# Expert loops with the up products' inner channels along partitions: no transposes of gated rows, and weights copied by ScalarE and VectorE

## The chip, the cores and the metric

One NeuronCore of a Trainium2 chip runs the whole program. The metric is the device time of one execution in microseconds. TensorE, VectorE, ScalarE, GpSimd and SyncE each run their own instruction stream and meet at semaphores. The profile calls them PE (its weight loads PEld), DVE, ACT, POOL and SP.

## The reference

Four sequences of 1024 tokens with 128 channels go through a mixing layer, a softmax attention, the mixing layer again, an expert layer, a linear attention and the expert layer again. The change is in the expert layer, which runs twice. Cut to what matters, for each token it computes:

```
up = moe_linear(xf, ids, w_up)            # 128 -> 512 channels, by the token's expert
u, gate = jnp.split(up, 2, axis=-1)       # two halves of 256
h = u * jax.nn.silu(gate)
down = moe_linear(h, ids, w_down)         # 256 -> 128 channels
```

Each token picks 2 of 8 experts, and all of it is float32.

## The kernel before, in words

The tokens are cut in rounds of 20, 12, 16 and 16 tiles of 128 tokens (SIZES); rounds 0 and 1 are the first pass through the expert layer, 2 and 3 the second. In each round every token's row is scattered twice to slots in HBM that are sorted by expert and padded to whole tiles of 128 rows, so that a tile has one expert. That gives 47, 31, 39 and 39 tiles, 156 in all. A loop (pe_loop, dve_loop, act_loop, pool_loop, sp_loop, one per engine) walks over them in units of two tiles: 24, 16, 20 and 20 units, 80 in all, the last of each round with one tile. The expert's weights lie in SBUF for all experts side by side (`k.expert_w`, in the trace `stack`), and a tile finds its expert's columns by an offset that a value_load (TENSOR_LOAD, with ISA instructions for registers) fetches from `moe_offsets`.

Iteration u of PE's loop does, in this order:

- loads the two offsets of unit u, and `turn(u)`: two transposes of the gathered rows (L1745) into bank 0; DVE scales them to `d.gt` (L1827, the trace calls the buffers lin_scores);
- side pieces of `k.e_plan` (first), which are other stages' work at fixed places: the end of the first attention and mixing, routing of the next round, preparation of the linear attention, and adding up the results of the round before (L1623, L1625);
- `up(u-1)`: for each tile one product with `d.gt` as weights (stationary) and 512 columns of the expert's up weights as moving operand (L1755). Its result has tokens along partitions. ACT takes silu of the gate half (L1861), DVE multiplies (L1834) into `d.h`;
- side pieces (second);
- `turn_hidden(u-2)`: four transposes of `d.h` (L1767) into bank 6, which ACT copies to `d.ht` (L1867);
- `down(u-3)`: four products of 128 columns (L1781) into bank 7, which ACT copies out (L1874). SP stores them to `results` (L1929) and, in its own order, loads the slots of units ahead (L1923).

SP's loads of the next round stand behind the last store of this one. POOL sends the scatters of the next round (L1689) and the gathers of the round before (L1700) as side pieces, and before each waits for PE to reach the same slot of the plan (pool_follow). Each engine takes its work in program order, so an iteration is as long as the slowest of what must be done in it. Between round 1 and round 2 lies the linear attention. After round 3 its 32 last gathers follow.

The key lines of the part that goes away, in pe_loop and act_loop:

```
instruction = T.transpose(k.ps[:, bank, at:at + P], d.h[:, u % NB, i, c * P:(c + 1) * P], k.ident[:, :])
...
A.activation(d.ht[:, u % NB, 0:width, :].rearrange("p i c -> p (i c)"), k.ps[:, bank, 0:width * HIDDEN],
             ACT_FN.Copy).then_inc(k.free[bank], 1)
```

## Time and profile before

| | |
|---|---|
| median of 3 runs | 1231.58 us (1227.18 to 1231.7) |
| the profiled execution: its own time / its span | 1228.77 us / 1227.0 us |
| PE busy | 1023.1 us, 83% |
| ACT busy | 798.9 us, 65% |
| DVE busy | 602.1 us, 49% |
| POOL busy | 428.5 us, 35% |
| first and last up product (L1755) of rounds 0 and 1 | from 633 us to 788 us |
| the same of rounds 2 and 3 | from 1030 us to 1171 us |

The span is from the first to the last instruction, the own time has what lies around it. Busy PE is not yet bound PE: matmuls overlap, and their ends are modelled. The chain of work that ended last says more: in it each piece stands with the time that it alone held up the end. A group of instructions has a count (x), a mean and the idle time before it with what ended it.

### The profile page before, as it was taken

Reading aid. Unit: us, or ns where it says so; the run is one execution under the profiler, and the core shown is the slowest. Engines: PE = TensorE matmul, PEld = TensorE weight load, DVE = VectorE, ACT = ScalarE, POOL = GpSimd, SP = SyncE. Lnnn points to the kernel's source line nnn. Section 1 sums busy time; section 2 is a strip of 40 time slices with the busy share of each in tenths; the row PEclk is TensorE's granted clock in tenths of the full one; section 3 lists DMA queues with packets and bytes.
Section 4 is the critical chain, followed back from the end, with each engine's and each line's share of the span. In section 5 each row is a group of like instructions: output and inputs, shape, how many; then the busy total and the mean of one; then the engine's idle time right before and its main releaser. Section 6 shows DMA issues by size and latency. Waiting matters only on the chain.

```text
span 1227.0 us, 22947 instructions
## 1 busy us (share of the span) xinstructions
PE 1023.1 (83%) x8718; PEld 474.0 (39%) x8718; DVE 602.1 (49%) x1791; ACT 798.9 (65%) x1164; POOL 428.5 (35%) x406
## 2 busy tenths in 40 slices
PE   4479998998999989999978989888889875989930
PEld 3342222322222233222236656644445443665620
DVE  4753565366365234321234525757877943524522
ACT  4439888988899979999953646665455522565510
POOL 4211122221111211454211345544543483455445
PEclk9679999999999999999999989989999987998975
DMA  5180280027127600300101333200000011334422
GB/s 153 39 130 1 52 116 3 2 50 106 15 53 115 187 1 1 126 26 27 31 14 52 98 107 93 80 21 20 17 16 2 14 42 45 108 104 114 121 69 67
DMA packets 84826, 74.74 MB, mean 61 GB/s; under 512 B 11440, under 2 KB 78896, under 8 KB 83824
## 3 DMA queue, kind: packets, MB, share of 16 engines
q1 hardware_dynamic: 74924, 55.48, 19.9%
q0 software_dynamic: 8192, 16.79, 4.7%
q8 instruction: 74, 1.21, 0.4%
q10 hardware_dynamic: 1604, 0.99, 0.3%
q14 instruction: 32, 0.26, 0.1%
HBM read 39.28 MB, written 33.95 MB: 60 GB/s over the span
## 4 chain that ended last, share of the span: by engine, by line
PE 55%; DVE 18%; ACT 12%; POOL 5%; issue 4%; DMA 1%; ACTq 0%; POOLq 0%; SPq 0%; DVEq 0%
PE ps L1035 11%; PE ps L1755 11%; ACT attn_probs L1307 10%; PE ps L1018 6%; PE ps L779 6%; PE ps L1781 5%; PE ps L615 3%; PE ps L1767 2%; POOL moe_back L1700 2%; PE ps L2063 2%; DVE lin_scores L2191 2%; PE ps L1745 2%; PE ps L1987 2%; PE ps L2077 1%; DVE stats L571 1%
## 5 line engine op out<-in xcount | busy, mean ns | idle before, releaser
L1307 ACT ACTIVATE attn_probs<-ps 128x1024 f32<-128x1024 f32 x512 | 484.6, 1063 | 48.1 <-PE ps L1018 46.8
L1035 PE MATMUL ps<-attn_probs,attn_v 128*18 128x512 f32 x2048 | 271.9, 603 | 4.5 <-DVE room L1266 3.9
L1689 POOL DMA_INDIRECT slots<-moe_xr,moe_slot x128 | 125.9, 984 | 141.5 <-ACT attn_probs L1307 51.8
L1018 PE MATMUL ps<-stack 50*128 50x512 bf16 x1024 | 165.5, 387 | 7.4 <-ACT attn_probs L1307 1.3
L1700 POOL DMA_INDIRECT moe_back<-results,moe_slot x128 | 123.6, 965 | 103.8 <-PE ps L1745 43.4
L1755 PE MATMUL ps<-stack,lin_scores 128*128 x312 | 155.4, 621 | 0.0
L1018 PEld LDWEIGHTS ps<-stack 50*128 50x128 bf16 x1024 | 34.3, 94 | 242.9 <-ACT attn_probs L1307 229.1
L1861 ACT ACTIVATE lin_scores<-ps 128x256 f32<-128x256 f32 x156 | 58.4, 382 | 97.8 <-PE ps L1755 97.8
L1834 DVE TENSOR_TENSOR lin_scores<-ps,lin_scores 128x256 f32<-128x256 f32 x156 | 59.0, 419 | 113.7 <-ACT lin_scores L1861 113.6
L1781 PE MATMUL ps<-stack,lin_scores 128*128 x624 | 83.6, 276 | 4.8 <-ACT lin_heads_out L1874 4.8
L1781 PEld LDWEIGHTS ps<-stack,lin_scores 128*128 128x128 f32 x624 | 76.0, 192 | 6.5 <-issue 6.5
L1755 PEld LDWEIGHTS ps<-stack,lin_scores 128*128 128x128 f32 x312 | 56.0, 200 | 40.2 <-issue 40.1
L1035 PEld LDWEIGHTS ps<-attn_probs,attn_v 128*18 128x18 f32 x2048 | 45.7, 97 | 59.8 <-issue 39.0
L1345 POOL TENSOR_TENSOR room<-room 128x512 f32<-128x512 f32 x16 | 22.2, 1389 | 132.8 <-DVE room L1131 132.8
L2261 ACT ACTIVATE lin_scores<-ps 128x512 f32<-128x512 f32 x64 | 34.7, 595 | 42.1 <-PE ps L2063 42.1
L2191 DVE TENSOR_TENSOR lin_scores<-ps,c_causal 128x512 f32<-128x512 f32 x64 | 41.0, 682 | 35.2 <-PE ps L2063 35.2
L1827 DVE TENSOR_SCALAR lin_scores<-ps,c_norm_scale 128x256 f32<-128x256 f32 x80 | 37.9, 474 | 35.0 <-PE ps L1745 34.6
L1767 PEld LDWEIGHTS ps<-c_ident,lin_scores 128*128 128x128 f32 x312 | 38.5, 142 | 37.6 <-issue 35.0
L1131 DVE SCALAR_TENSOR_TENSOR room<-ps,c_attn_b,moe_xr 128x512 f32<-128x512 f32 x32 | 23.9, 749 | 58.9 <-PE ps L779 57.4
L1867 ACT ACTIVATE lin_scores<-ps 128x512 f32<-128x512 f32 x80 | 46.7, 584 | 7.6 <-PE ps L1767 4.8
L571 DVE BATCH_NORM_STATS2 stats<-x 128x6 f32<-128x128 f32 x192 | 41.4, 278 | 20.2 <-POOL x L897 8.8
L1745 PE MATMUL ps<-c_ident,moe_gathered 128*128 128x128 f32 x156 | 33.0, 294 | 20.0 <-DMA moe_gathered<-slots 13.1
(227 smaller groups left out, 1483.0 us busy)
## 6 DMA issues: line engine op xcount, KB each, us to landing
moe_gathered<-slots SPq DMA_DIRECT2D x76, 128.0 KB, 2.4
results<-lin_heads_out SPq DMA_DIRECT2D x76, 128.0 KB, 1.8
stack<-qk_parts SPq DMA_DIRECT2D x36, 256.0 KB, 9.4
qk_parts<-moe_xr SPq DMA_DIRECT2D x32, 128.0 KB, 2.5
qk_parts<-moe_xr SPq DMA_DIRECT2D x16, 192.0 KB, 2.8
stack<-in_expert_w SPq DMA_DIRECT2D x1, 3072.0 KB, 10.6
slots<-zeros SPq DMA_DIRECT2D x1, 3008.0 KB, 11.3
slots<-zeros SPq DMA_DIRECT2D x1, 2496.0 KB, 18.3
```

The lines of the kernel that those rows point to most:

```text
L779: instruction = T.matmul(out[cols, :], weights[:, cols], moving, start=True, stop=True)
L1018: instruction = T.matmul(k.ps[:, SCORE_BANKS[i % 3][s], :], d.stack[b % 2][rows, 1, pair, kt * P:(kt + 1) * P], d.stack[b % 2][rows, 0, pa ...
L1035: instruction = T.matmul(k.ps[32 * j:32 * j + STRIP, PV_BANK, :], d.v[:, b % 2, kt, first:first + STRIP], d.probs[:, n % A_PROBS, j * BANK ...
L1307: A.activation(d.probs[:, n % A_PROBS, 2 * e * BANK:2 * (e + 1) * BANK], k.ps[:, banks[0]:banks[1] + 1, :].rearrange("p a n -> p (a n)"), ...
L1689: G.indirect_dma_start(out=k.dram["slots"][half][0:SLOT_TILES[r] * P], out_offset=bass.IndirectOffsetOnAxis(ap=d.slot[:, FIRST[r] + at, c: ...
L1700: G.indirect_dma_start(out=k.back[:, i % RING, c, :], out_offset=None, in_=k.dram["results"][half][0:SLOT_TILES[r] * P], in_offset=bass.In ...
L1755: T.matmul(k.ps[:, bank, :], d.gt[:, u % NB, i, :], w[:, bass.ds(offset[u, i], 2 * HIDDEN)], start=True, stop=True).then_inc(k.full[bank], 1)
L1767: instruction = T.transpose(k.ps[:, bank, at:at + P], d.h[:, u % NB, i, c * P:(c + 1) * P], k.ident[:, :])
L1781: instruction = T.matmul(k.ps[:, bank, i * DIM:(i + 1) * DIM], d.ht[:, u % NB, i, c * P:(c + 1) * P], w[:, 2 * HIDDEN + c * DIM:][:, bass. ...
L1834: V.tensor_tensor(d.h[:, u % NB, i, :], k.ps[:, bank, 0:HIDDEN], d.silu[:, u % NB, i, :], ALU.mult).then_inc(k.free[bank], 1)
L1861: A.activation(d.silu[:, u % NB, i, :], k.ps[:, bank, HIDDEN:2 * HIDDEN], ACT_FN.Silu).then_inc(k.e_silu, 1)
L2191: V.tensor_tensor(d.scores[:, m % NS, :].rearrange("p (j t) -> p j t", j=HPG), k.ps[:, bank, :].rearrange("p (j t) -> p j t", j=HPG), caus ...
```

## The change

The up product is turned round. The expert's up weights, 128 columns at a time, become the weights (stationary), and `d.gt` becomes the moving operand of 128 columns: four products a tile (UP_CHUNKS) in the place of one of 512 columns. The result has inner channels along partitions, which is what the down product needs as weights, so `turn_hidden` and its copy fall away on PE and ACT, and `down` reads `d.h`. A stationary operand isn't addressed by an offset from a register here: so `weights(u)` copies 512 columns of each tile to a fixed buffer, the first tile of a unit on ACT, the second on DVE, and each of the two loads its own offset from `moe_offsets`. `down` comes two iterations behind (DOWN_LAG) where it was three, and has two banks (6 and 7) in turn.

```diff
-SIDE_BANK = 1
+SIDE_BANK, DOWN_BANKS, DOWN_LAG = 1, (6, 7), 2
...
             bank, n = k.use["eup", r, u, i]
             if n and u < NB:
                 T.wait_ge(k.free[bank], n)
-            T.matmul(k.ps[:, bank, :], d.gt[:, u % NB, i, :], w[:, bass.ds(offset[u, i], 2 * HIDDEN)], start=True,
-                     stop=True).then_inc(k.full[bank], 1)
-
-    def turn_hidden(u):
-        bank, n = k.use["eht", r, u]
-        if n:
-            T.wait_ge(k.free[bank], n)
-        for i in range(unit_width(r, u)):
-            u_bank, u_n = k.use["eup", r, u, i]
-            T.wait_ge(k.free[u_bank], u_n + 1)
-            for c in range(2):
-                at = i * HIDDEN + c * P
-                instruction = T.transpose(k.ps[:, bank, at:at + P], d.h[:, u % NB, i, c * P:(c + 1) * P], k.ident[:, :])
-        instruction.then_inc(k.full[bank], 1)
+            if i == 0:
+                T.wait_ge(k.e_weights_act, UNITS_BEFORE[r] + u + 1)
+            else:
+                T.wait_ge(k.e_weights_dve, PAIRS_BEFORE[r] + u + 1)
+            for c in range(UP_CHUNKS):
+                instruction = T.matmul(k.ps[:, bank, c * P:(c + 1) * P], d.up[u % NB][i][:, c * P:(c + 1) * P],
+                                       d.gt[:, u % NB, i, :], start=True, stop=True)
+            instruction.then_inc(k.full[bank], 1)
...
+    def weights(u):
+        if unit_width(r, u) < UNIT:
+            return
+        if u >= NB:
+            bank, n = k.use["eup", r, u - NB, UNIT - 1]
+            V.wait_ge(k.full[bank], n + 1)
+        offset = V.value_load(k.moe.offsets[0:1, r % 2, u * UNIT + 1:u * UNIT + 2], min_val=0,
+                              max_val=(EXPERTS - 1) * EXPERT_COLS)
+        V.tensor_copy(d.up[u % NB][1], w[:, bass.ds(offset, 2 * HIDDEN)]).then_inc(k.e_weights_dve, 1)
...
+    def weights(u):
+        offset = A.value_load(k.moe.offsets[0:1, r % 2, u * UNIT:u * UNIT + 1], min_val=0,
+                              max_val=(EXPERTS - 1) * EXPERT_COLS)
+        A.activation(d.up[u % NB][0], w[:, bass.ds(offset, 2 * HIDDEN)], ACT_FN.Copy).then_inc(k.e_weights_act, 1)
...
         if 0 <= u - 1 < UNITS[r]:
             silu(u - 1)
+        if 1 < u + 1 < UNITS[r]:
+            weights(u + 1)
         for piece in second:
             side(piece)
-        if 0 <= u - 2 < UNITS[r]:
-            turn_hidden(u - 2)
-        if 0 <= u - 3 < UNITS[r]:
-            down(u - 3)
+        if 0 <= u - DOWN_LAG < UNITS[r]:
+            down(u - DOWN_LAG)
```

On DVE `weights(u + 1)` stands ahead of `hidden(u - 1)`; both engines copy for unit 0 ahead of their loop, ACT for unit 1 too.

PE's order in one iteration of round 0 before the change, without the two offset loads of L1791 that open and close it (ISA rows set registers):

```order
L1745 MATMUL ps<-c_ident,moe_gathered 128x128 x2
L1755 ISA
L1755 MATMUL ps<-stack,lin_scores 128x512
L1755 ISA
L1755 MATMUL ps<-stack,lin_scores 128x512
L1767 MATMUL ps<-c_ident,lin_scores 128x128 x4
L1781 ISA
L1781 MATMUL ps<-stack,lin_scores 128x128
L1781 ISA
L1781 MATMUL ps<-stack,lin_scores 128x128
```

PE's order in such an iteration of the changed kernel, in which L1760 is the up product, L1774 the down product and L1784 the offset load:

```order
L1784 TENSOR_LOAD moe_offsets
L1784 ISA x2
L1784 TENSOR_LOAD moe_offsets
L1784 ISA x2
L1745 MATMUL ps<-c_ident,moe_gathered 128x128 x2
L1760 MATMUL ps<-lin_scores 128x128 x4
L1760 MATMUL ps<-lin_scores,lin_sums 128x128 x4
L1774 ISA
L1774 MATMUL ps<-stack,lin_scores 128x128
L1774 ISA
L1774 MATMUL ps<-stack,lin_scores 128x128
```

The four transposes are gone, and eight products of 128 columns stand where two of 512 stood. The offset loads stay, since the down product still needs them.

ACT's order in one iteration before:

```order
L1861 ACTIVATE lin_scores<-ps 128x256 x2
L1867 ACTIVATE lin_scores<-ps 128x512
L1874 ACTIVATE lin_heads_out<-ps 128x256
L1861 ACTIVATE lin_scores<-ps 128x256 x2
L1867 ACTIVATE lin_scores<-ps 128x512
```

And in the changed kernel, where L1883 is silu, L1877 the copy of weights and L1889 the copy of the down product:

```order
L1883 ACTIVATE lin_scores<-ps 128x256 x2
L1875 TENSOR_LOAD moe_offsets
L1875 ISA x2
L1877 ISA
L1877 ACTIVATE lin_scores<-stack 128x512
L1889 ACTIVATE lin_heads_out<-ps 128x256
L1883 ACTIVATE lin_scores<-ps 128x256 x2
```

A copy of 512 columns has gone and another has come, with an offset load ahead of it.

DVE's order at the start of round 0, as a piece of the difference (L1827 becomes L1818, which scales the turned rows; L1184 and L1188 are the end of the first attention):

```order
-L2169 TENSOR_SCALAR lin_hide<-c_ident 128x128
-L2171 TENSOR_SCALAR lin_later<-c_causal 128x512
-L1827 TENSOR_SCALAR lin_scores<-ps,c_norm_scale 128x256
+L2186 TENSOR_SCALAR lin_hide<-c_ident 128x128
+L2188 TENSOR_SCALAR lin_later<-c_causal 128x512
+L1838 TENSOR_LOAD moe_offsets
+L1838 ISA x2
+L1840 ISA
+L1840 COPY lin_scores<-stack 128x512
+L1818 TENSOR_SCALAR lin_scores<-ps,c_norm_scale 128x256
 L1184 RECIPROCAL attn_inv<-ps 128x16 x2
```

An offset load and a copy now stand ahead of the scaling and of the attention's last pieces.

## Rows read from the trace of the kernel before

**Rows 1.** The page's head: the span.

```profile
span 1227.0 us, 22947 instructions
```

**Rows 2.** Chain of work, round 2: start us, us, what.

```profile
1047.16 1.72 PE ps L1755 x4
1048.88 0.44 PE ps L1767 x4
1049.32 0.89 PE ps L1781 x8
1050.21 0.22 PE ps L1745 x2
```

**Rows 3.** Timeline of PE, two turns of round 2, ten units apart.

```profile
1057.13 0.38 PE L1745 MATMUL ps<-c_ident,moe_gathered 128*128 128x128 f32 x2
...
1089.81 0.38 PE L1745 MATMUL ps<-c_ident,moe_gathered 128*128 128x128 f32 x2
```

**Rows 4.** Busy time by window: us, PE, PEld, DVE, ACT, POOL busy (x), PEclk, DMA.

```profile
632.00:650.00 18.00, 14.58 (x65) 8.90 (x64) 9.65 (x30) 6.75 (x14) 3.34 (x3) 0.93 0.13 38
...
733.00:785.00 52.00, 50.49 (x251) 32.58 (x250) 31.63 (x105) 29.56 (x71) 30.91 (x32) 0.96 0.34 95
```

**Rows 5.** Timeline of PE in the set-up, short products back to back.

```profile
78.40 0.38 PE L692 MATMUL ps<-attn_probs,mix_xt 128*128 128x128 f32 x2
...
80.18 1.06 PE L698 MATMUL ps<-c_mix_w,attn_probs 128*128 128x128 f32 x8
```

**Rows 6.** Groups by line and form, ACT: busy us, mean ns, idle before.

```profile
L1861 ACT ACTIVATE lin_scores<-ps 128x256 f32<-128x256 f32 x156 | 58.4, 382 | 97.8 <-PE ps L1755 97.8
L1867 ACT ACTIVATE lin_scores<-ps 128x512 f32<-128x512 f32 x76 | 45.2, 595 | 7.6 <-PE ps L1767 4.8
...
L2227 ACT ACTIVATE room<-room 128x512 f32<-128x512 f32 x16 | 10.0, 630 | 0.0
```

**Rows 7.** Groups by line and form, DVE.

```profile
L1834 DVE TENSOR_TENSOR lin_scores<-ps,lin_scores 128x256 f32<-128x256 f32 x156 | 59.0, 419 | 113.7 <-ACT lin_scores L1861 113.6
...
L1827 DVE TENSOR_SCALAR lin_scores<-ps,c_norm_scale 128x256 f32<-128x256 f32 x76 | 36.5, 480 | 34.2 <-PE ps L1745 33.8
...
L1625 DVE SCALAR_TENSOR_TENSOR x<-moe_back,moe_weight,x 128x128 f32<-128x128 f32 x64 | 23.0, 360 | 2.3
...
L2126 DVE TENSOR_SCALAR room<-room 128x512 f32<-128x512 f32 x16 | 7.2, 453 | 0.2 <-ACT room L2227 0.2
```

**Rows 8.** Timeline of PE at the start of round 0: idle before in brackets.

```profile
630.95 0.66 PE L1745 MATMUL ps<-c_ident,moe_gathered 128*128 128x128 f32 x2 [0.80 <-issue]
```

**Rows 9.** Timeline at the start of round 0, DVE beside POOL.

```profile
625.82 1.64 POOL L2597 MEMSET lin_v<- 128x1728 f32 x1 [28.62 <-PE ps L1035]
...
626.39 1.53 DVE L2169 TENSOR_SCALAR lin_hide<-c_ident 128x128 bf16<-128x128 f32 x1
```

**Rows 10.** Timeline in the linear attention, an indirect DMA of POOL and DVE beside it.

```profile
856.95 0.96 POOL L1700 DMA_INDIRECT moe_back<-results,moe_slot  x1 [3.20 <-PE ps L2077]
857.59 0.56 DVE L2126 TENSOR_SCALAR room<-room 128x512 f32<-128x512 f32 x1
```

**Rows 11.** Chain of work, end of round 0 and first load of round 1.

```profile
725.12 0.39 ACT lin_heads_out L1874
...
725.64 1.17 PE ps L1781 x8
...
726.83 0.39 ACT lin_heads_out L1874
...
727.35 0.72 PE ps L1781 x4
...
728.84 2.06 DMA moe_gathered<-slots
```

**Rows 12.** Timeline of POOL, first and last of 32 scatters in round 2.

```profile
1051.81 1.19 POOL L1689 DMA_INDIRECT slots<-moe_xr,moe_slot  x1 [24.45 <-DVE moe_slot L1597]
...
1098.82 0.97 POOL L1689 DMA_INDIRECT slots<-moe_xr,moe_slot  x1 [0.30 <-issue]
```

More of the change, by code:

```diff
@@ L50 @@
 TILES_BEFORE, SLOTS_BEFORE, UNITS_BEFORE = (sums_before(counts) for counts in (SIZES, SLOT_TILES, UNITS))
+PAIRS_BEFORE = sums_before([tiles // UNIT for tiles in SLOT_TILES])
 LOOP_TILES = 16
@@ L528, in plan_loop @@
                 k.banks.fill(key, SIDE_BANK)
-        if 0 <= u - 2 < UNITS[r]:
-            k.banks.fill(("eht", r, u - 2), 6)
-        if 0 <= u - 3 < UNITS[r]:
-            k.banks.fill(("edown", r, u - 3), 7)
+        if 0 <= u - DOWN_LAG < UNITS[r]:
+            k.banks.fill(("edown", r, u - DOWN_LAG), DOWN_BANKS[(u - DOWN_LAG) % 2])
 def all_banks_free(E, k, stage):
@@ L1779, in down @@
         for i in range(unit_width(r, u)):
+            u_bank, u_n = k.use["eup", r, u, i]
+            T.wait_ge(k.free[u_bank], u_n + 1)
             for c in range(2):
-                instruction = T.matmul(k.ps[:, bank, i * DIM:(i + 1) * DIM], d.ht[:, u % NB, i, c * P:(c + 1) * P],
+                instruction = T.matmul(k.ps[:, bank, i * DIM:(i + 1) * DIM], d.h[:, u % NB, i, c * P:(c + 1) * P],
                                        w[:, 2 * HIDDEN + c * DIM:][:, bass.ds(offset[u, i], DIM)], start=c == 0,
@@ L1835, in hidden @@
                             ALU.mult).then_inc(k.free[bank], 1)
+    w = k.expert_w.rearrange("p e c -> p (e c)")
+    V.wait_ge(k.e_offsets, r + 1)
+    V.wait_ge(k.expert_in, 16)
+    def weights(u):
[7 more added lines that the diff above has]
+        V.tensor_copy(d.up[u % NB][1], w[:, bass.ds(offset, 2 * HIDDEN)]).then_inc(k.e_weights_dve, 1)
+    weights(0)
     for u in range(UNITS[r] + 3):
@@ L1846, in dve_loop @@
             side(piece)
+        if u == 0:
+            if r == 0:
+                bank, n = k.use["turn", BATCH - 1, HALVES - 1]
+                V.wait_ge(k.full[bank], n + 1)
+            weights(1)
 def act_loop(A, k, r):
@@ L1861, in silu @@
             A.activation(d.silu[:, u % NB, i, :], k.ps[:, bank, HIDDEN:2 * HIDDEN], ACT_FN.Silu).then_inc(k.e_silu, 1)
-    def turn_hidden(u):
-        bank, n = k.use["eht", r, u]
-        A.wait_ge(k.full[bank], n + 1)
-        width = unit_width(r, u)
-        A.activation(d.ht[:, u % NB, 0:width, :].rearrange("p i c -> p (i c)"), k.ps[:, bank, 0:width * HIDDEN],
-                     ACT_FN.Copy).then_inc(k.free[bank], 1)
     def down(u):
@@ L1875, in down @@
                      ACT_FN.Copy).then_inc(k.free[bank], 1)
+    weights(0)
+    weights(1)
     for u in range(UNITS[r] + 3):
@@ L1882, in act_loop @@
             silu(u - 1)
+        if 1 < u + 1 < UNITS[r]:
+            weights(u + 1)
         for piece in second:
             side(piece)
-        if 0 <= u - 2 < UNITS[r]:
-            turn_hidden(u - 2)
-        if 0 <= u - 3 < UNITS[r]:
-            down(u - 3)
+        if 0 <= u - DOWN_LAG < UNITS[r]:
+            down(u - DOWN_LAG)
 def pool_follow(G, k, r, u, second):
@@ L1945, in sp_loop @@
             side(piece)
-        if 0 <= u - 3 < UNITS[r]:
-            store(u - 3)
+        if 0 <= u - DOWN_LAG < UNITS[r]:
+            store(u - DOWN_LAG)
         for piece in second:
@@ L2424, in loop_buffers @@
     d.gt = room[:, 3 * NB, :].rearrange("p (b i c) -> p b i c", b=NB, i=UNIT)
-    d.silu, d.h, d.ht = (room[:, i * NB:(i + 1) * NB, :].rearrange("p b (i c) -> p b i c", i=UNIT) for i in range(3))
+    d.silu, d.h = (room[:, i * NB:(i + 1) * NB, :].rearrange("p b (i c) -> p b i c", i=UNIT) for i in range(2))
+    d.up = [(room[:, 2 * NB, :], room[:, 2 * NB + 1, :]), (room[:, 3 * NB + 1, :], sums[:, :, :].rearrange("p s n -> p (s n)"))]
     return d
@@ L2493, in macaron_kernel @@
             k.lin = linear_buffers(nc, late, k)
-            k.loop = loop_buffers(nc, late, k.lin.scores, k.lin.heads_out)
+            k.loop = loop_buffers(nc, late, k.lin.scores, k.lin.heads_out, k.lin.sums)
             k.back = late.enter_context(nc.sbuf_tensor("moe_back", [P, RING, TOPK, DIM], F32))
@@ L2526, in macaron_kernel @@
         k.expert_in = signal("expert_in")
-        k.e_xr, k.e_both, k.e_gap, k.e_gap_act, k.e_slots, k.e_offsets, k.e_silu, k.e_kept, k.e_merged = (
-            signal("e_" + n) for n in ("xr", "both", "gap", "gap_act", "slots", "offsets", "silu", "kept", "merged"))
+        k.e_xr, k.e_both, k.e_gap, k.e_gap_act, k.e_slots, k.e_offsets, k.e_silu, k.e_kept, k.e_merged, k.e_weights_act, k.e_weights_dve = (
+            signal("e_" + n) for n in ("xr", "both", "gap", "gap_act", "slots", "offsets", "silu", "kept", "merged", "weights_act", "weights_dve"))
         k.e_gather, k.e_store, k.e_back = signals("e_gather", NG), signals("e_store", NG), signals("e_back", RING)
```

12 lines of the change are left out of this document (6 added, 6 removed).

## The prediction

> **What bounds the kernel now.** I read the chain of waits first. In the steady part of an expert loop it lies on PE alone: two up products 1.72 us, four transposes of hidden rows 0.44, four down products (eight records, since each float32 product is two) 0.89, two turns 0.22, and the next unit begins [rows 2]. That is 3.27 us a unit without a hole. The timeline gives the same over a long stretch: 32.68 us for ten units [rows 3]. Of the 76 spacings between turns inside the four loops I count 46 at 3.26 to 3.30 us. The others have side products in them, or a wait.
>
> The windows tell where PE isn't the bound [rows 4]. At the start of round 0 PE is busy in 14.58 of 18 us: there a chain through DVE, POOL and ACT ends the first attention and the mixing. In round 1 it is 50.49 of 52, with DVE busy for 31.63 and ACT for 29.56. So PE sets the pace, and what counts is PE's work in a unit, and whether ACT and DVE keep a shorter pace.
>
> **The change, PE's part.** Removed: four transposes, 0.44 us a unit, or 0.22 a tile [rows 2]. Added: the up product of a tile was 0.86 us and becomes four float32 products of 128 columns, each with its own weights, eight records. The down product has this form, eight in 0.89 us [rows 2]. Sixteen such records, and then eight more, run without a hole in the set-up: the first begins at 78.40, the next group at 80.18, so 1.78 us for sixteen [rows 5]. A tile so costs 0.89 and not 0.86. The sum is 0.22 less 0.03, 0.19 us a tile, and a unit takes 2.89 us (0.22 + 1.78 + 0.89). Over 156 tiles (the count of L1861 [rows 6]) that is 29.6 us.
>
> **What this meets on ACT.** A unit on ACT is two silus of 382 ns, a copy of 595 and a down copy as long as a silu: 1.74 us [rows 6]. The copy from PSUM goes, and one of 512 columns from SBUF comes, 630 ns by the nearest row, L2227. New is the offset load ahead of it. No row shows one on ACT. On PE two loads with their ISAs fill a hole of 0.80 us when nothing covers them [rows 8], 0.4 each. Its bounds are nothing, if the instruction ahead hides it, and 0.8, if the two on PE overlapped. With 0.4, ACT has 2.2 us of 2.89. The copy for unit u+1 begins when up(u-1) is done and is needed after down(u-2), a turn, up(u), down(u-1) and another turn, 4.0 us later. Only the down copy queues behind it, and its bank is the other one now.
>
> **On DVE.** It had 0.48 (L1827) and twice 0.42 (L1834), and gets a load and a copy. The copy's nearest row is L2126, one source in SBUF, 453 ns [rows 7]. That makes 1.77 us, with the load 2.2. Queued behind it is `hidden(u-1)`, for which down(u-1) waits: from the end of up(u-1) PE has 2.89 us of other work (down 0.89, turn 0.22, up 1.78), and load, copy and two multiplies take 1.7. It holds, with 1.2 to spare. Where a tile is added up (rounds 1 and 3, 32 units), two instructions of about 0.36 join: 2.9 us against 2.89. There DVE is level with PE.
>
> The Trainium skill has a price for the load (DMA: Bandwidth & Descriptors, Latency and other measured facts): a floor of about 600 ns for a tensor_load. The pair in 0.80 us here is cheaper than that. By the page DVE would need 3.1 us in those 32 units, and some 7 us of the gain would go.
>
> DVE's copy also meets POOL's indirect DMAs. Beside one, L2126 took 0.56 us where its mean is 0.45 [rows 7, 10]. Beside a memset of POOL, one DVE instruction took 1.53 us [rows 9]. The loops' POOL work is nearly all indirect DMA, so I add 0.1 us a copy, 8 us in all on DVE, of which most lies beside PE. The Trainium skill (SBUF — State Buffer, SBUF: two separate sides) says that a two-port DVE instruction and a GpSimd one lock each other out for the whole instruction. The memset row agrees. The DMA row lost a tenth, not a whole instruction, so the row decides.
>
> **Where the gain is not paid out.** In about 12 of the 80 units PE waits for a chain of others, so 0.38 each is lost: 4.6 us. At the start of round 0 a load and a copy, 0.85 us, stand ahead of DVE's scaling and of the attention's last pieces, on the chain there, and again twice in the mixing that follows: 2.5 us. For the level DVE in 32 units and for late pieces I take 4.5 us (0.14 each). Its bounds are 0, and 12 if DVE falls 0.38 behind in each and the gain of these units is lost.
>
> **Where more is paid.** At a round's end down products wait for the one bank: after L1781 x8 PE waits through 0.39 us of ACT, sends eight in 1.17 us (not 0.89), waits again for 0.39, and sends the last four in 0.72 us (not 0.44) [rows 11]. SP's load of the next round stands behind the last store. With two banks, and without the transposes' copy, both waits and both overhangs go (0.39 + 0.39 + 0.28 + 0.28), 1.3 us for each of four rounds, 5.2 in all. Small holes before the turn in rounds 1 and 3, when PE's queue waits for ACT's copy and its offset loads come late, give perhaps 1.5.
>
> **The sum.** 29.6 - 4.6 - 2.5 - 4.5 + 5.2 + 1.5 = 24.7 us less. The profiled execution took 1.8 us more than its span of 1227.0 [rows 1], 1228.8, and is 2.8 below the median of the runs. 1228.8 - 24.7 is 1204, and I say **1205**, a little towards the median.
>
> **The rivals.**
>
> *PE keeps the pace* (the forecast), chance 0.62, 1195 to 1214. For it: the chain is all PE, and the form of the new products is measured.
>
> *DVE or ACT takes over in part*, chance 0.22, 1213 to 1223. An offset load costs 0.8 us on DVE, and the copies wait for POOL. DVE then needs 2.6 us in plain units and 3.3 in the 32 with additions, where nothing is gained (12 us less gain). For it: DVE is busy for 31.63 of 52 us in round 1 [rows 4], and 16 copies and loads add 14 to 20 when the window should shrink by 6. Against it: other rounds have little on DVE.
>
> *The scatters hold the round's end*, chance 0.05, about 1208 by round 2. 32 scatters begin at 1051.81, the last at 1098.82 [rows 12], paced by PE. Back to back they are 1.27 us apart, 41 us, and PE's part shrinks from 47 to 41. It is level, so some 0 to 4 us, inside the forecast's range.
>
> *Slower: loads stall ACT*, chance 0.07, about 1245. An offset load whose engine has to run empty first would cost ACT the load alone. From 1.5 us on, ACT's 1.77 us and the load reach PE's old 3.27. At 1.7 it is 3.47, which is 0.2 times 80 units, 16 us slower. Against it: PE hides two such loads behind its products in 46 units.
>
> *Slower: PE's queue loses its lead*, chance 0.04, about 1255. Before, the long up products give PE's sequencer time to run ahead and fetch the offsets. All products are short now. If the pair's 0.80 us [rows 8] opens in each unit, it is 3.69 us, 34 less 5 slower. It decides from 0.38 us of hole a unit. Against it: 24 short records without a hole [rows 5], though with no load among them.
>
> **How the numbers follow.** About 0.5%, 6 us, is what a measurement here can tell from no change. The range is **1194 to 1222**: the low end is the whole 29.6 with the ends' 5.2 and little lost (1228.8 - 34.8), the high end the second rival's. Faster 0.86 (the first three cases' 0.89, less 0.03 that falls inside 6 us), same 0.04 (that and 0.01 of the slower ones), slower 0.10.
>
> **What would show it.** In the changed trace: the turns' spacing in round 2 near 2.89 us, and eight up records in 0.89. L1877 near 630 ns, L1840 near 453 to 560. PE idle before the turn near nothing: if it is there with "issue" before it, the sequencer's rival is right. DVE's idle time before L1825 gone in rounds 1 and 3 would be the second rival. The load of round 1 (SP) would begin 8 to 11 us sooner, that of round 3 by 8 to 10 us against its own loop's start. The forecast is wrong if an offset load on ACT or DVE costs over 1 us, or if short products in long rows run slower than 0.111 us a record.

## The result, and the profile after

The changed kernel takes 1224.82 us (median of 16 runs, 1222.22 to 1229.81) where the kernel before takes 1230.18 (16 runs beside them): ratio 0.9963, 95% interval 0.9951 to 0.9976, a gain of some 5 us. The forecast was 1205. The profiled execution has a span of 1220.3 us. The page of the changed kernel, busy time and chain by engine:

```profile
PE 990.8 (81%) x9310; PEld 531.4 (44%) x9342; DVE 626.2 (51%) x1867; ACT 797.9 (65%) x1164; POOL 429.2 (35%) x406
...
PE 50%; DVE 19%; ACT 11%; POOL 7%; issue 5%; DMA 2%; DVEq 0%; ACTq 0%; POOLq 0%
```

PE lost 32 us of busy time and the span only 6.7. In the steady part the unit of PE is as forecast. The chain of work in round 3 answers to [rows 2]:

```profile
1125.79 0.22 PE ps L1745 x2
1126.01 1.79 PE ps L1760 x16
1127.79 0.89 PE ps L1774 x8
1128.68 0.22 PE ps L1745 x2
```

A unit takes 2.89 us, without a hole. The groups by line answer to [rows 6, 7]; L1877 and L1840 are ACT's and DVE's copies of weights, L1825 is DVE's multiply with the silu (L1834 before), L1745 the turn:

```profile
L1825 DVE TENSOR_TENSOR lin_scores<-ps,lin_scores 128x256 f32<-128x256 f32 x156 | 58.5, 416 | 12.2 <-ACT lin_scores L1883 12.2
...
L1877 ACT ACTIVATE lin_scores<-stack 128x512 f32 x80 | 50.4, 631 | 21.2 <-issue 19.1 <-PE ps L1035 2.0
...
L1745 PE MATMUL ps<-c_ident,moe_gathered 128*128 128x128 f32 x156 | 33.3, 295 | 26.8 <-DMA moe_gathered<-slots 14.6 <-issue 6.7 <-DVE lin_scores L1818 5.4
...
L1840 DVE COPY lin_scores<-stack 128x512 f32 x40 | 17.5, 438 | 53.5 <-PE ps L1760 38.3 <-issue 14.4 <-DVE moe_scored L1567 0.8
...
L1840 DVE COPY lin_sums<-stack 128x512 f32 x36 | 15.7, 437 | 37.3 <-PE ps L1760 31.1 <-issue 5.4 <-DVE moe_scored L1567 0.8
```

The sizes of the copies are those forecast (631 and 438 ns). Before, DVE sat idle for 113.6 us until a silu was there [rows 7], now for 12.2 (first row). The idle time has not vanished: 90.8 us of it now stand ahead of the copies (the two L1840 rows), 69.4 of them until the up products end. `weights(u + 1)` waits until up(u-1) is done, because it overwrites that unit's buffer, and only then loads and copies. So the load and the copy begin at the same moment as the silu, and `hidden(u-1)` stands behind them.

The table is worked out from the rows of the turns (L1745 in the changed kernel) of one trace each, us: when the first begins, from the first to the last of each round (r0 to r3), and what lies between and behind. Two kinds of chips met the sets. On the first (first measurement, third and fifth set) the kernel before takes 1230 us, on the second (first, second and fourth set of experiments) 1243 to 1246.

| kernel | first turn | r0 | gap | r1 | to r2 | r2 | gap | r3 | rest |
|---|---|---|---|---|---|---|---|---|---|
| before | 626.2 | 93.4 | 11.4 | 52.8 | 239.2 | 70.1 | 12.3 | 62.6 | 59.0 |
| changed, first trace | 626.2 | 96.4 | 9.2 | 53.5 | 240.8 | 71.4 | 10.3 | 56.3 | 56.2 |
| e10 changed | 626.9 | 96.9 | 9.5 | 53.1 | 240.9 | 72.0 | 10.1 | 56.5 | 56.2 |
| e11 ACT in some units | 629.1 | 91.6 | 8.7 | 51.7 | 238.3 | 66.8 | 10.0 | 56.5 | 56.2 |
| e12 no DVE copy | 625.9 | 86.4 | 9.3 | 48.8 | 240.2 | 65.5 | 10.2 | 54.7 | 56.2 |
| e18 all on ACT | 627.7 | 91.4 | 9.8 | 50.7 | 240.2 | 66.0 | 10.1 | 55.0 | 56.2 |
| *second kind:* e5 changed | 627.7 | 97.9 | 9.7 | 52.7 | 253.8 | 78.8 | 11.9 | 59.0 | 56.2 |
| e6 PE padded | 627.2 | 106.4 | 9.5 | 54.8 | 249.9 | 83.0 | 10.8 | 59.2 | 56.3 |
| e7 load twice | 628.8 | 107.5 | 9.2 | 57.0 | 247.4 | 87.0 | 11.9 | 63.8 | 56.2 |
| e8 ACT in some units | 629.1 | 90.9 | 9.6 | 53.8 | 253.3 | 71.5 | 12.4 | 58.4 | 56.2 |
| e16 changed | 626.9 | 99.0 | 11.1 | 54.4 | 249.6 | 80.9 | 11.8 | 59.5 | 56.2 |
| e13 copy, no load | 627.2 | 91.6 | 11.6 | 52.0 | 248.7 | 74.3 | 13.1 | 57.2 | 56.2 |
| e14 load, no copy | 627.8 | 92.6 | 10.3 | 52.4 | 248.2 | 74.5 | 12.8 | 57.5 | 56.2 |

Of the rounds only round 3 paid out: 6.3 us less, and 2.8 behind it; the two gaps gave 2.2 and 2.0. Rounds 0, 1 and 2 became longer (3.0, 0.7, 1.3 us), though PE has 0.38 us less to do in each of their 60 units. Rounds 0 and 2 carry the routing of the next round, a long row of small DVE steps with PE, POOL and ACT in between, and round 0 the end of the attention and the mixing too.

The chain of work at the start of round 0 shows what stands there now; "q" marks an engine's sequencer, so the DVEq rows are the offset load with its register instructions:

```profile
631.90 1.71 PE ps L779 x8
633.61 2.22 PE ps L1760 x16
635.83 0.03 issue
635.86 0.30 DVEq L1838
636.16 0.04 issue
636.19 0.18 DVEq L1838
...
636.57 0.43 DVE lin_scores L1840
636.99 0.66 DVE lin_scores L1825 x2
```

The up products end at 635.83, the multiply begins at 636.99, 1.16 us later: 0.74 for the load, 0.43 for the copy. The silu, 0.39 us in the chain of e12 below, runs beside them and is no longer seen.

### The profile page after: what moved, and what is told of

It reads as the page before. It is cut to its first block, busy times and chain, and to the rows that moved or that the text cites. A ratio compares the mean times of both kernels' runs of the same rounds, so it can differ in the third digit from the quotient of the medians.

```text
span 1220.3 us, 24717 instructions
## 1 busy us (share of the span) xinstructions
PE 990.8 (81%) x9310; PEld 531.4 (44%) x9342; DVE 626.2 (51%) x1867; ACT 797.9 (65%) x1164; POOL 429.2 (35%) x406
## 4 chain that ended last, share of the span: by engine, by line
PE 50%; DVE 19%; ACT 11%; POOL 7%; issue 5%; DMA 2%; DVEq 0%; ACTq 0%; POOLq 0%
PE ps L1035 11%; ACT attn_probs L1307 10%; PE ps L1760 9%; PE ps L1018 6%; PE ps L779 6%; PE ps L1774 4%; POOL moe_back L1700 3%; PE ps L615 3%; PE ps L2080 2%; DVE lin_scores L2208 2%; PE ps L1745 2%; PE ps L2004 1%; PE ps L2094 1%; DVE stats L571 1%; POOL slots L1689 1%
## 5 line engine op out<-in xcount | busy, mean ns | idle before, releaser
L1689 POOL DMA_INDIRECT slots<-moe_xr,moe_slot x128 | 125.8, 983 | 142.4 <-DVE moe_slot L1597 53.9
L1760 PE MATMUL ps<-lin_scores 128*128 128x128 f32 x960 | 127.6, 286 | 0.0
L1883 ACT ACTIVATE lin_scores<-ps 128x256 f32<-128x256 f32 x156 | 58.3, 380 | 100.0 <-PE ps L1760 99.7
L1760 PEld LDWEIGHTS ps<-lin_scores 128*128 128x128 f32 x960 | 120.9, 202 | 1.2 <-issue 0.8
L1774 PE MATMUL ps<-stack,lin_scores 128*128 x624 | 84.6, 278 | 1.9 <-DVE lin_scores L1825 1.9
L1774 PEld LDWEIGHTS ps<-stack,lin_scores 128*128 128x128 f32 x624 | 77.0, 194 | 3.6 <-issue 3.5
L1825 DVE TENSOR_TENSOR lin_scores<-ps,lin_scores 128x256 f32<-128x256 f32 x156 | 58.5, 416 | 12.2 <-ACT lin_scores L1883 12.2
L1877 ACT ACTIVATE lin_scores<-stack 128x512 f32 x80 | 50.4, 631 | 21.2 <-issue 19.1
L2278 ACT ACTIVATE lin_scores<-ps 128x512 f32<-128x512 f32 x64 | 34.7, 595 | 41.7 <-PE ps L2080 41.7
L1745 PE MATMUL ps<-c_ident,moe_gathered 128*128 128x128 f32 x156 | 33.3, 295 | 26.8 <-DMA moe_gathered<-slots 14.6
L615 PE MATMUL ps<-c_ident,room 128*128 128x128 f32 x132 | 24.2, 312 | 29.1 <-issue 10.0
L779 PE MATMUL ps<-room,c_qk_w 128*32 128x256 f32 (+1 forms) x416 | 41.3, 404 | 6.2 <-DVE attn_heads_out L1188 4.2
## 6 DMA issues: line engine op xcount, KB each, us to landing
slots<-zeros SPq DMA_DIRECT2D x1, 3008.0 KB, 11.9
```

Source lines behind the costliest of these rows:

```text
L615: instruction = T.transpose(k.ps[:, bank, i * P:(i + 1) * P], source(i), k.ident[:, :])
L779: instruction = T.matmul(out[cols, :], weights[:, cols], moving, start=True, stop=True)
L1689: G.indirect_dma_start(out=k.dram["slots"][half][0:SLOT_TILES[r] * P], out_offset=bass.IndirectOffsetOnAxis(ap=d.slot[:, FIRST[r] + at, c: ...
L1760: instruction = T.matmul(k.ps[:, bank, c * P:(c + 1) * P], d.up[u % NB][i][:, c * P:(c + 1) * P], d.gt[:, u % NB, i, :], start=True, stop= ...
L1774: instruction = T.matmul(k.ps[:, bank, i * DIM:(i + 1) * DIM], d.h[:, u % NB, i, c * P:(c + 1) * P], w[:, 2 * HIDDEN + c * DIM:][:, bass.d ...
L1825: V.tensor_tensor(d.h[:, u % NB, i, :], k.ps[:, bank, 0:HIDDEN], d.silu[:, u % NB, i, :], ALU.mult).then_inc(k.free[bank], 1)
```

## The experiments

**Theory A**: DVE's load and copy stand in the serial chains of rounds 0 to 2, between the end of the up products and the multiply, and that ate the gain. **Theory B**: in those rounds PE's time no longer counts, because the chain through DVE, POOL and DMA is the bound whatever is copied where. The first set's texts have another theory B (PE itself loses the time, with short products and offset loads that come late) and a theory C (ACT's copy costs it).

### First set: without a yardstick

e1_no_dve_copy. DVE neither loads nor copies, PE doesn't wait for it, and both tiles use the first one's weights.

```
-        if unit_width(r, u) < UNIT:
-            return
+        return
...
-                instruction = T.matmul(k.ps[:, bank, c * P:(c + 1) * P], d.up[u % NB][i][:, c * P:(c + 1) * P],
+                instruction = T.matmul(k.ps[:, bank, c * P:(c + 1) * P], d.up[u % NB][0][:, c * P:(c + 1) * P],
```

> Left out: VectorE's offset loads and copies (76 of each); the second tile of a unit multiplies with the first tile's weights, so TensorE's work is unchanged. Theory A (VectorE's load of 0.7 us and copy of 0.43 stand in its serial chain wherever routing, mixing or additions run, about 10 us on the chain of waits directly, and start late scatters behind them): 10 to 18 us less than the changed kernel, near 1210. Theory B (the loss comes from TensorE: short products that lose the sequencer's lead, offset loads that come late): within 3 us of the changed kernel, 1222 to 1228. Theory C (ScalarE's copy and the side pieces behind it): also within 3 us.

e2_dve_fixed_offset. DVE copies, with a fixed offset.

```
-        offset = V.value_load(k.moe.offsets[0:1, r % 2, u * UNIT + 1:u * UNIT + 2], min_val=0,
-                              max_val=(EXPERTS - 1) * EXPERT_COLS)
-        V.tensor_copy(d.up[u % NB][1], w[:, bass.ds(offset, 2 * HIDDEN)]).then_inc(k.e_weights_dve, 1)
+        V.tensor_copy(d.up[u % NB][1], w[:, 0:2 * HIDDEN]).then_inc(k.e_weights_dve, 1)
```

> Left out: VectorE's 76 offset loads; it copies the weights of expert 0 for every second tile, the copy itself stays. Theory A with the load as the larger part (0.70 of 1.13 us each): 6 to 11 us less than the changed kernel. If the copies themselves are what costs: 2 to 5 us less. Theories B and C: within 2 us.

e3_all_on_act. ACT loads and copies for both tiles.

```
+        for i in range(unit_width(r, u)):
...
+            offset = A.value_load(k.moe.offsets[0:1, r % 2, u * UNIT + i:u * UNIT + i + 1], min_val=0,
+                                  max_val=(EXPERTS - 1) * EXPERT_COLS)
+            A.activation(d.up[u % NB][i], w[:, bass.ds(offset, 2 * HIDDEN)], ACT_FN.Copy).then_inc(k.e_weights_act, 1)
```

> Both tiles' weights are copied by ScalarE, VectorE copies none. Theory A: VectorE's chains are as before, 10 us less there; ScalarE needs 0.76 + 0.24 + 1.26 + 0.38 = 2.64 us in a plain unit of 2.90, and 4.3 where it also keeps rows (every second unit in parts of all rounds, 16 units), so some 5 to 10 us are lost again: 1213 to 1222. Theory C (ScalarE is what costs): slower than the changed kernel by over 5 us.

e4_dve_copy_late. DVE copies after the multiply and the second side pieces of the iteration.

```
-        if 1 < u + 1 < UNITS[r]:
-            weights(u + 1)
         if 0 <= u - 1 < UNITS[r]:
             hidden(u - 1)
         for piece in second:
             side(piece)
+        if 1 < u + 1 < UNITS[r]:
+            weights(u + 1)
```

> VectorE's load and copy for unit u+1 stand behind the products of silu and the second side pieces instead of ahead of them. Theory A, the position ahead of hidden is what costs: 3 to 8 us less than the changed kernel, as the load no longer delays what the down product and the second pieces wait for. If VectorE's time itself is the limit in these chains, wherever the copy stands: within 2 us of the changed kernel.

Measured, ratio to the kernel before (1246.01 us on this chip): e1 0.9960 (0.9935 to 0.9985), e2 0.9950 (0.9927 to 0.9974), e3 0.9944 (0.9919 to 0.9968), e4 1.0003 (0.9986 to 1.0019). Read against 0.9963 they say that DVE's part costs nothing, and they misled me: the changed kernel itself had not run on this chip, and the next set shows that its ratio isn't the same on such a chip. What this set is worth is said behind the fourth.

### Second set: the slopes

e5_after_again is the changed kernel.

> The changed kernel itself, with nothing but a comment added, on the chip on which the other three of this set run. Both theories expect a ratio of 0.994 to 0.998 to the kernel before, as first measured (0.9963). It is the yardstick for the three others: what counts for them is their distance from this run.

Measured 1249.57 us, before 1243.04, ratio 1.0064 (1.004 to 1.0088): outside what both theories gave. The next three are read against 1249.57.

e6_pe_padded_r02. 0.22 us of PE more a tile in rounds 0 and 2.

```
-            for c in range(UP_CHUNKS):
+            for c in ([0] if r in PADDED else []) + list(range(UP_CHUNKS)):
```

> The changed kernel, in which the first 128 columns of each up product are computed twice in rounds 0 and 2 (0.22 us more of PE a tile, 0.44 a unit, about what the removed transposes took); 42 units, 18.5 us of PE more. Theory A (PE's time is still passed on; what ate the gain is DVE's load and copy, which stand in the serial chain of the routing): each step of that chain runs through a unit of PE, so nearly all of it shows: 13 to 18 us slower than the changed kernel, ratio to before about 1.007 to 1.011. Theory B (in rounds 0 and 2 the chain through DVE, POOL and DMA has become the bound and PE's time no longer counts, so the saving on PE is not paid out there, with or without DVE's copy): under 6 us slower than the changed kernel, ratio to before at most 1.001.

e7_dve_load_twice. DVE loads an offset that it doesn't use ahead of each that it does.

```
+        V.value_load(k.moe.offsets[0:1, r % 2, u * UNIT:u * UNIT + 1], min_val=0,
+                     max_val=(EXPERTS - 1) * EXPERT_COLS)
         offset = V.value_load(k.moe.offsets[0:1, r % 2, u * UNIT + 1:u * UNIT + 2], min_val=0,
```

> The changed kernel, in which DVE loads an offset it doesn't use ahead of the one that it does, in every pair (76 loads more, 0.3 to 0.7 us each, the copy as it was). Theory A: about 14 of them stand in the serial chain of rounds 0 and 2 and another 10 in round 1, so 8 to 14 us slower than the changed kernel, ratio to before 1.003 to 1.008. Theory B: the loads lie beside PE or beside POOL, 0 to 4 us slower, ratio to before 0.996 to 0.9995.

e8_act_in_chain_units. ACT loads and copies for both tiles in the units that carry routing or mixing.

```
+BOTH_ON_ACT = [set(range(0, 14)), {0, 1} | set(range(8, UNITS[1])), set(range(0, 13)), {0}]
...
-        if unit_width(r, u) < UNIT:
+        if unit_width(r, u) < UNIT or u in BOTH_ON_ACT[r]:
             return
...
+        for i in range(unit_width(r, u) if u in BOTH_ON_ACT[r] else 1):
```

> The changed kernel, but in the units in which DVE carries the routing or the mixing (units 0 to 13 of round 0, 0, 1 and 8 to 15 of round 1, 0 to 12 of round 2) ACT loads both offsets and copies both tiles' weights; DVE keeps its own elsewhere. Theory A: DVE's 1.1 us a unit leave the chain of waits in some 12 places, 6 to 12 us faster than the changed kernel, ratio to before 0.987 to 0.991. Theory B: PE, POOL and the scatters set the time there, so within 3 us of the changed kernel, ratio 0.994 to 0.998.

Measured: e6 1258.94, 9.4 us more than the changed kernel. Both theories missed it (13 to 18, under 6). By the table 8.5 us appeared in round 0 of the 10.3 added (47 tiles), and 4.2 in round 2 of 8.6. PE's time counts by half to four fifths there, so B in its plain form is out. These are single traces: the changed kernel's own (e5 and e16) differ by 1.1 us in round 0 and 2.1 in round 2, and the stretch between rounds 1 and 2 was 3.9 us shorter in e6 than in e5, so the total understates it. e7 1270.63, 21.1 more, where A had 8 to 14 and B 0 to 4: 0.28 us for each of 76 loads, in all four rounds (9.6, 4.3, 8.2 and 4.8, while the stretch between rounds 1 and 2 was 6.5 shorter). That is too much for the 24 loads that A had on the chain: DVE's time counts in many more units, those of round 3 too. e8 1237.06, 12.5 less (A 6 to 12, B within 3): 7.0 of it in round 0 and 7.3 in round 2. That is A, and more than A had.

### Third set: on a chip like the first

e9_before_traced is the kernel before, e10_after_third the changed one, e11 is e8's kernel, e12 is e1's.

> The kernel before itself, for a trace of it beside those of the changed one on the same chip. On the chips of the first two sets the changed kernels show stops of 3.7 to 6.9 us on ACT in the linear-attention stage that the first trace of the changed kernel has not (25 us on the chain there). If they belong to the chip, this trace has them too, 15 to 25 us from the last turn of round 1 to the first of round 2 on top of 239.2. If they belong to the changed kernel, this trace has none, and the stage takes 239 to 242 us.

> The changed kernel, unchanged, a third time, since its ratio was 0.9963 on the first chip and 1.0064 on another. If the difference lies in the chip's stops, the ratio follows them: near 0.996 where the linear-attention stage takes about 241 us, near 1.006 where it takes about 254. Theory A and theory B say nothing on this; it is the yardstick for the next two.

> The kernel in which ACT copies both tiles' weights in the units that carry the routing and the mixing, again. Theory A: 6 to 12 us faster than the changed kernel of this set, with round 0 at 89 to 92 us and round 2 at 68 to 73 from first to last turn. If its 12.5 us of the last set came from a disturbance of that set's yardstick and not from the chain: within 3 us.

> The changed kernel in which DVE copies nothing and loads no offset; both tiles of a unit are multiplied with the weights of the first (so part of the experts' weights is left out of the computation), ACT as it was, PE's work the same in amount. Theory A: 10 to 16 us faster than the changed kernel of this set, at least as fast as the kernel in which ACT takes the copies over. Theory B (what bounds is PE's clock, POOL and the scatters): within 3 us of the changed kernel.

Measured: e9 1229.6 (ratio 1.0001, 0.9989 to 1.0013), e10 1225.16 (0.9955, 0.9938 to 0.9972), e11 1210.95 (0.9835, 0.9816 to 0.9855), e12 1199.95 (0.9771, 0.9749 to 0.9792). Without DVE's load and copy the kernel is 25.2 us faster than the changed one, 30 faster than before. With ACT doing them where DVE is in the chain it is 14.2 faster. Both are beyond the ranges that A gave. B is refuted, and so are the first set's B and C: e12 leaves PE's work and ACT's as they were. On chips of the second kind e12's kernel had 0.9960 (e1) and e11's 0.9956 (e8).

The chain of e12 at the place shown above, its up products being L1758, silu L1880 and multiply L1823:

```profile
633.06 2.35 PE ps L1758 x16
635.41 0.02 issue
635.43 0.39 ACT lin_scores L1880
635.82 0.02 issue
635.85 0.76 DVE lin_scores L1823 x2
```

From products to multiply it is 0.44 us and not 1.16, so this passage costs the chain 0.72 us. The passages aren't alike: in the next one the load partly lies beside DVE's instruction ahead of it. The chain of e10 holds 13 such copies (7 in round 0, 2 in round 1, 4 in round 2), with their loads 11.4 us (the issue pieces between them not counted). That isn't yet 25. A second part is in the clock; windows of round 2 in the changed kernel (e10), and in e12:

```profile
1026.00:1098.00 72.00, 59.90 (x477) 57.52 (x478) 39.84 (x129) 35.16 (x84) 28.17 (x27) 0.89 0.29 87
```

```profile
1010.00:1076.00 66.00, 57.43 (x487) 55.89 (x488) 32.42 (x105) 35.36 (x85) 29.16 (x28) 0.93 0.33 96
```

The granted clock (third figure from the end) is 0.89 of 2.4 GHz in the one and 0.93 in the other. Round 2 alone doesn't carry the point: the changed kernel's first trace has 0.92 there, and the kernel before, from its own first turn on (1023 to 1095), 0.93. Single stretches show it better. In the changed kernel's first trace, in round 0, and then in e12:

```profile
650.62 1.25 PE ps L779 x2
651.88 3.26 PE ps L1760 x16
```

```profile
648.13 1.10 PE ps L779 x2
649.23 1.78 PE ps L1758 x16
```

Sixteen records in 3.26 us and not in 1.78: the granted clock is 0.50 (1.2 GHz) from 651.43 to 654.84 us, and 1.00 in e12 at the same place. Ahead of it PE had stood idle for 1.43 and then 2.20 us, waiting for DVE in the mixing, where e12 has 0.62 and 1.56. Over the whole span the granted clock is 0.926 in e10 and 0.933 in e12. If all that lacks is time at half the clock, that is 181 and 160 us, 20 more in the changed kernel (an estimate from these clocks and the spans of 1222.1 and 1197.3). Over the whole run the up products of e10, and of e12, were busy for:

```profile
L1760 PE MATMUL ps<-lin_scores 128*128 128x128 f32 x960 | 128.7, 287 | 0.0
...
L1760 PE MATMUL ps<-lin_scores,lin_sums 128*128 128x128 f32 x288 | 39.6, 282 | 0.0
```

```profile
L1758 PE MATMUL ps<-lin_scores 128*128 128x128 f32 x1248 | 157.2, 280 | 0.0
```

That is 168.3 against 157.2 us for the same 1248 records, 11.1 us. How much of it counts in the end, and how much only shortens a wait, these sums don't tell.

### Fourth set: load or copy

A copy that slows others through its port would be another cause than DVE's time. e13 is e2's kernel, e14 has the load and no copy (both tiles use the first one's weights), e15 is e8's kernel with units 0 and 1 of round 0 as in the change, and e16 the changed kernel. The first line is what e14 leaves out, the others are e15 against e8.

```
-        V.tensor_copy(d.up[u % NB][1], w[:, bass.ds(offset, 2 * HIDDEN)]).then_inc(k.e_weights_dve, 1)
...
-BOTH_ON_ACT = [set(range(0, 14)),
+BOTH_ON_ACT = [set(range(2, 14)),
```

> The changed kernel with DVE's copy but without its offset load: the second tile of a pair is multiplied with the up weights of the first expert (this part of the computation is changed). If DVE's time as such counts, the load's 0.70 us of 1.13 us a pair is taken away: some 60% of the 25 us between the changed kernel and the one without copies, 13 to 17 us faster than the changed kernel (ratio to before 0.982 to 0.985 where the changed kernel is at 0.996). If it is the copy, by its port, that slows others: 0 to 6 us faster.

> The changed kernel with DVE's offset load but without its copy (both tiles of a unit are multiplied with the weights of the first, a part of the computation is changed). If DVE's time as such counts: 8 to 12 us faster than the changed kernel (ratio 0.986 to 0.990). If it is the copy that slows others: 19 to 25 us faster (ratio 0.976 to 0.981).

> As the kernel in which ACT takes over the copies of the units with routing and mixing, but units 0 and 1 of round 0 as in the change (DVE copies its half). ACT's copies for these stood ahead of its last exponentials of the attention, which set the end there; the first turn of round 0 should come at 626 to 627 us again and not at 629, and the time be 1 to 3 us less: ratio 0.981 to 0.983. The result stays the reference's. If the 629 has another cause: no difference, 0.9835.

> The changed kernel unchanged, the yardstick for this set: ratio 0.996 on a chip on which ACT has no long stops in the linear-attention stage, 1.006 on one that has them.

Measured, before at 1242.79: e16 1251.3 (1.0084, 1.0053 to 1.0115), e13 1233.93, 17.4 less (0.9934, 0.9912 to 0.9955), e14 1237.18, 14.1 less (0.9969, 0.9941 to 0.9997), e15 1238.43, 12.9 less (0.9968, 0.9951 to 0.9985). The expected ratios were for the other kind of chip. By distance from e16, e13 is at the upper edge of what DVE's time gives (13 to 17) and e14 above it (8 to 12), and neither is near what a slowing copy would give (0 to 6, and 19 to 25). (e14's twelve runs lie between 1233.06 and 1247.92, so its 14.1 is rough.) Nor did DVE's copies slow POOL: its scatters (L1689) took 984 ns before and 983 in the changed kernel. The chains of e13 and of e14 between products and multiply:

```profile
637.92 0.43 DVE lin_scores L1838
638.34 0.74 DVE lin_scores L1825 x2
```

```profile
638.34 0.30 DVEq L1836
...
638.67 0.18 DVEq L1836
...
638.96 0.76 DVE lin_scores L1823 x2
```

From products to multiply it is 0.45 us in e13, 0.65 in e14, 0.44 in e12 with neither and 1.16 with both. The copy alone fits beside the silu, the load alone nearly, and only together do they stand out. Longer units say the same. From the turn of unit 5 of round 0 to the next it is 8.72 us in e10, 7.08 in e16, 6.45 in e12 and e13 and 6.66 in e14; for unit 7 of round 1 it is 7.09, 6.94, 5.42, 5.73 and 5.70. This is why the two savings (17.4 and 14.1) sum to more than that of both.

With the yardsticks of the second kind (e5 1.0064, e16 1.0084) the first set can be read after all, as an estimate across chips. It is allowed in so far as e2 and e13, one kernel on two chips of this kind, have 0.9950 and 0.9934. Against these yardsticks e1 is 13 to 15 us faster than the changed kernel, no more than e13 or e14 alone; e2 14 to 17, e3 15 to 17, and e4, where the copy only comes later, 8 to 10. Why leaving out both gives less there than the 25.2 us of the first kind stays open.

e15 is as e8 against its yardstick (12.5 and 12.9), its first turn came at 628.5, so neither the first turn nor the time changed, where 1 to 3 us less were expected. What starts round 0 later in e8 and e11 stays open.

### Fifth set: the best kernel

> The kernel before, unchanged, for its trace. Where the kernel before takes 1240 us or more: the stops on ACT in the linear-attention stage are there too (from the last turn of round 1 to the first of round 2 248 us or more, where 239 were first seen), and its rounds take 1 to 3 us more than 93.4, 52.8, 70.1 and 62.6. Where it takes 1230: no such stops, the stages as first seen.

> The changed kernel with all up weights loaded and copied by ACT, nothing of it on DVE. By DVE's time in the chain of waits: like the kernel in which ACT takes over only some units, ratio 0.980 to 0.987 where the kernel before takes 1230 us, and 0.992 to 0.998 where it takes 1240 or more. If ACT (a copy of 0.63 us more a unit, 2.6 of 2.9 us) becomes the bound in rounds 1 and 3: these two rounds 1 to 3 us longer than with ACT in some units only.

Measured on a chip of the first kind: e17 1229.46 (0.9995, 0.9981 to 1.0009), so its question, what the kernel before does on a chip of the second kind, wasn't met; e18, which is e3's kernel, 1208.3, ratio 0.982 (0.9806 to 0.9834), 22 us faster than before and 17 faster than the changed kernel by their ratios. Rounds 1 and 3 (50.7 and 55.0) are shorter than e11's (51.7 and 56.5), so ACT is no bound. It leaves nothing of the computation out, and is faster than both kernels.

## Why the prediction was wrong

Its direction was right and its amount wrong: 5 us gained, 24.7 forecast.

- *PE's part, 2.89 us a unit*: right, shown by the chain of round 3. A tile's eight records take 0.89 us.
- *ACT's part*: right. The copy took 631 ns, and even the copying of both tiles (e18) fits.
- *Round ends*: right at the end of round 3. The changed kernel's chain behind the last turn, answering to [rows 11]:

```profile
1167.98 0.89 PE ps L1774 x8
1168.88 0.23 issue
1169.11 0.72 PE ps L1774 x4
1169.83 0.02 issue
1169.85 0.29 ACT lin_heads_out L1889
```

  The two waits of 0.39 us and the first overhang are gone. The second stays: four records of the last tile still take 0.72 us and begin after 0.23. The whole stretch behind the last turn gave 2.8 us. At the ends of rounds 0 and 2 something else came last. The chain of the changed kernel at the end of round 0:

```profile
724.42 0.96 POOL slots L1689
...
725.68 3.99 DMA slots<-moe_xr,moe_slot
729.67 0.02 issue
729.69 2.09 DMA moe_gathered<-slots
```

  SP's load of the next round now waits until the last scatter has landed, and no longer for the last store. In the trace before, the load began 0.78 us after the last down product of round 0 and 1.03 after that of round 2. By these rows it could have begun at 729.06 and 1104.23 us here; it began at 729.69 and 1105.71, so the scatters took back some 2 us (an estimate) of the 5.2 that were forecast for the ends. The chain of e12 goes through them at both ends, that of e10 only at the end of round 2. PE's holes before the turn, for which 1.5 us of gain were forecast, grew instead (issue before L1745, 4.2 to 6.7 us).
- *The sum without DVE*: right in total. Leave out the two terms for DVE (2.5 and 4.5) and the forecast is 31.7 us less than before; e12, where DVE does nothing of the change, is 30 less. That it comes so near is in part luck, since two terms in it, the ends and the small holes, did not come as forecast.
- **The step that failed** is the cost of DVE's load and copy: "At the start of round 0 a load and a copy, 0.85 us, stand ahead of DVE's scaling [...] and again twice in the mixing that follows: 2.5 us. For the level DVE in 32 units and for late pieces I take 4.5 us". 7.0 us were forecast, 25.2 measured (e10 less e12). By the table 10.5 of them lie in round 0, 4.3 in round 1, 6.5 in round 2, 1.8 in round 3, and 1.8 in the stretches between and ahead. Three things were off in it. The load takes 0.74 us where DVE stood idle until the up products ended, not 0.4, near the upper bound of 0.8. The places were 3 and are 13 on the chain of e10, since the routing in rounds 0 and 2 passes through a multiply again and again, and the 12 waiting units were priced only for what PE doesn't gain there, not for what DVE adds. And PE spends more time at half its clock (0.50 in the stretch above), which no term held.
- *"It holds, with 1.2 to spare"* was right for PE's steady units, and the wrong test for DVE: what counted in a chained unit wasn't down(u-1), but the side piece that queues behind the multiply.
- *Loads at the level DVE, bound 12*: round 3, with additions in 16 units, gained 6.3 of 7.2 us (19 spacings by 0.38 us). By the table 6.1 of the 25.2 us lie in rounds 1 and 3, which hold the 32 units, not far from the 4.5 that they had, and 17.0 lie in rounds 0 and 2.
- *The rivals*. "DVE or ACT takes over in part" (0.22) came nearest, with 1213 to 1223 and the load at 0.8 us; but its 12 us lay in the 32 units with additions. The rows of round 3 rule it out as written and e12 puts most of the loss elsewhere. The scatters came true in part: they hold the round's end in the places shown above, for some 2 us. They are no part of the 25: in the chain of 1063 to 1108 L1689 has 8.6% in e10, and 8.6% in e12 too. Loads that stall ACT: no, ACT's load lies beside the silu (last section). PE's queue that loses its lead: 2.5 us in all and not 34. (That rival's own sum gives 1258 us, not 1255.)
- *The markers*: turns near 2.89 and L1877 near 630 came out, L1840 took 438 where 453 to 560 was said. The load of round 1 was to begin 8 to 11 us sooner; it began 0.85 us later (728.84 and 729.69). That was the sign that round 0 had gained nothing. The idle time before L1825 was named as a marker for rounds 1 and 3 only; it went in all rounds.

What stays open is how the 25.2 us divide between DVE's own delay, the clock, and POOL's and DMA's later starts, and what the second kind of chip does. The cheapest way out wasn't tried either: DVE's load ahead of its wait for the up products, so that it runs while DVE waits, or a third buffer, with which the copy needn't wait for them either.

On the second kind all traces of the changed kernels show stops without a releaser, and on the first kind none does. The longest are on ACT in the linear attention (in e16 four of 3.7 to 6.9 us), shorter ones lie in the rounds too, so the rounds of the two kinds can't be compared; from e16:

```profile
1008.37 4.44 another core or an unknown queue
1012.81 0.02 issue
1012.83 0.61 ACT stack L2260
...
1027.88 0.38 ACT lin_sums L2286
1028.27 6.90 another core or an unknown queue
```

Against the first kind the kernel before loses about 13 us there in all and the changed one about 25. The holes by PE's sequencer before the turn were larger too, 9.3 and 11.3 us in e5 and e16 against 6.7 and 5.5. No trace of the kernel before was had on such a chip, so whether it has the same stops isn't known, nor why the ratio turns.

## What to carry to other kernels

Before work is given to an engine with idle time, look at what ends that idle time: DVE's 113.6 us were waits for the silu, short ones inside serial chains, and work put there delays everything behind it. Price an addition by every unit in which its engine is on a chain, side chains included, and not only by whether the main engine's slack covers it in steady state. Look where an offset load stands: ahead of a wait its time should be hidden, behind it it was in the chain (moving it was not tried here). Run the changed kernel itself in every set of experiments, since a ratio to the kernel before didn't carry from one kind of chip to the other.

## What the hardware showed unexpectedly

An offset load costs little where an instruction of its engine stands ahead of it. In the changed kernel it took, on DVE and on ACT (ns, least, median, most):

```profile
L1838 DVEq TENSOR_LOAD <-moe_offsets x76: 299/305/700, 625.8 to 1160.3; - x76
```

```profile
L1875 ACTq TENSOR_LOAD <-moe_offsets x80: 271/280/640, 625.8 to 1163.5; - x80
```

At 635.86 us both engines begin such a load. With its register instructions it takes 0.71 us on DVE until the copy begins, and 0.62 on ACT. But ACT has begun its silu at 635.85 and the load runs beside it, while DVE has nothing to do: its load stands behind the wait for the up products. In the chain of e12 only 0.34 us are left between the end of a silu and ACT's copy:

```profile
734.78 0.28 ACT lin_scores L1880
...
735.09 0.15 ACTq L1872
...
735.40 0.63 ACT lin_scores L1874
```

DVE's next copy (639.59 us), whose load runs beside instructions of DVE, likewise has only 0.35 us of idle time ahead of it. So most of the gap between 0.74 and 0.34 lies in what the engine was doing, and not in the engine. The Trainium skill (DMA: Bandwidth & Descriptors, Latency and other measured facts) gives a floor of about 600 ns for a tensor_load. The instruction itself is half of that here; only with its register instructions, until the copy begins, is it at that size.

DVE's copy was slowed a little by POOL's indirect DMAs. In the changed kernel's first trace the 28 copies that met one took 456 ns in the mean and 680 at most, the others 426 and at most 430, where I had added 0.1 us. A lock of one engine by the other for a whole instruction, as the Trainium skill (SBUF — State Buffer, SBUF: two separate sides) has it, isn't seen beside them here: the most that a copy lost is 0.25 us, and such a DMA instruction takes 0.98.
